# Splits of the next layer's weights moved to other steps of the vector engine, in a six-layer local-attention kernel

## The reference

```python
for i in range(DEPTH):                                   # 6
    x = attn_layer(shift_tokens(x), Wqkv[i], q_scale[i], k_scale[i], Wo[i]) + x
    x = ffn_layer(shift_tokens(x), ln_g[i], ln_b[i], W1[i], b1[i], W2[i], b2[i]) + x
```

## Time and profile before

| what | value |
|---|---|
| median of three runs | 3742.32 us |
| profiled execution, its own time | 3746.89 us |
| its span, first to last instruction | 3745.10 us |
| busy: TensorE, its weight loads, VectorE, ScalarE, GpSimd | 96%, 81%, 84%, 90%, 73% |
| mean granted TensorE clock | 0.99 |

### The profile page before, as it was taken

The page is one execution under the profiler, slowest core; times in us unless marked ns, Lnnn a source line. Parts: engine busy times, 40 slices in busy tenths (PEclk is TensorE's granted clock), DMA queues, the critical chain, the costliest instruction groups (busy, mean ns, idle before and its releaser), DMA issues.

```text
span 3745.1 us, 133069 instructions
## 1 busy us (share of the span) xinstructions
PE 3590.0 (96%) x47348; PEld 3050.9 (81%) x47348; DVE 3132.4 (84%) x7015; ACT 3369.8 (90%) x10919; POOL 2748.6 (73%) x2060
## 2 busy tenths in 40 slices
PE   7999979999999999999999999999999999999998
PEld 4666668888888888888888888888888888888887
DVE  7888978788887888888788888888888888788897
ACT  7888859989999899999899999899999999999996
POOL 0111249888788888888888788788888888888884
PEclk9999989999999999999999999999999999999999
DMA  2000001111121111111111111111111111111111
GB/s 99 7 7 16 7 21 45 35 32 34 38 49 34 37 31 32 43 43 38 32 32 38 38 45 37 32 32 39 39 44 34 32 32 44 34 35 37 40 37 38
DMA packets 164727, 132.71 MB, mean 35 GB/s; under 512 B 113901, under 2 KB 124781, under 8 KB 163821
## 3 DMA queue, kind: packets, MB, share of 16 engines
q1 hardware_dynamic: 164077, 124.19, 13.6%
HBM read 25.84 MB, written 4.19 MB: 8 GB/s over the span
## 4 chain that ended last, share of the span: by engine, by line
PE 73%; DVE 5%; ACT 5%; issue 4%; DVEq 0%; ACTq 0%; POOLq 0%; POOL 0%
PE bank L1015 10%; PE bank L971 10%; PE bank L996 8%; PE bank L1051 8%; PE bank L1035 6%; PE bank L933 4%; PE bank L934 4%; PE bank L935 4%; PE bank L894 4%; PE bank L1028 3%; ACT a_E L1343 2%; PE bank L867 2%; PE bank L869 2%; PE bank L868 2%; PE bank L947 2%
## 5 line engine op out<-in xcount | busy, mean ns | idle before, releaser
L1446 POOL TENSOR_TENSOR a_rn<-a_ssqc,a_minus_half 128x16 f32<-128x16 f32 x384 | 1113.9, 2901 | 514.9 <-DVE a_ssqc L1637 505.2
L1343 ACT ACTIVATE a_E<-bank,a_negmax 128x96 f32<-128x96 f32 x3072 | 1015.8, 363 | 23.6 <-DVE a_negmax L1586 23.0
L1467 POOL TENSOR_TENSOR a_r<-a_u,a_rn 128x512 f32<-128x512 f32 x768 | 789.7, 1049 | 0.6
L1454 POOL TENSOR_TENSOR a_PN<-a_E,a_erec 128x384 f32<-128x384 f32 x768 | 742.4, 987 | 11.5 <-PE bank L996 8.1
L1343 ACT ACTIVATION_READ_ACCUMULATOR a_E<-bank,a_negmax 128x1 f32 x3072 | 707.7, 230 | 0.0
L1326 ACT ACTIVATE a_QK<-bank 128x512 f32<-128x512 f32 x768 | 467.5, 609 | 130.2 <-PE bank L971 130.1
L1319 ACT ACTIVATE a_sq<-bank 128x512 f32<-128x512 f32 x768 | 483.9, 630 | 44.1 <-PE bank L935 12.6
L1599 DVE TENSOR_TENSOR a_u<-bank,a_rot_c 128x512 f32<-128x512 f32 x768 | 521.3, 679 | 2.4 <-ACT a_sq L1319 2.4
L1609 DVE TENSOR_TENSOR a_v<-bank,a_rot_s 128x512 f32<-128x512 f32 x768 | 521.8, 679 | 0.0
L971 PE MATMUL bank<-ident,a_r 128*128 128x128 f32 x3072 | 483.9, 280 | 18.9 <-DVE a_bias L1572 11.8
L1304 ACT ACTIVATE a_PT<-bank 128x512 f32<-128x512 f32 x758 | 479.7, 633 | 20.0 <-PE bank L996 16.3
(11 more groups left out here) (180 smaller groups left out, 8423.2 us busy)
## 6 DMA issues: line engine op xcount, KB each, us to landing
a_V_even<-a_V_odd SPq DMA_DIRECT2D x384, 128.0 KB, 2.3
a_V_even<-a_V_odd SPq DMA_DIRECT2D x192, 64.0 KB, 2.1
a_raw<-in_qkv SPq DMA_DIRECT2D x20, 384.0 KB, 3.6
a_x_sh<-X SPq DMA_DIRECT2D x48, 128.0 KB
a_V_even<-a_V_odd SPq DMA_DIRECT2D x192, 32.0 KB, 2.0
a_x_sh<-X SPq DMA_DIRECT2D x48, 127.0 KB
a_f_sh<-X SPq DMA_DIRECT2D x47, 128.0 KB
a_f_sh<-X SPq DMA_DIRECT2D x47, 127.0 KB
```

Of the source, the lines that this page charges most:

```text
L1343: ins = act.activation(E[:, s.par, k, :], scores[:, i % 2, col:col + KW], ACT.Exp, bias=negmax[:, s.par, k:k + 1], accum_out=esum[:, s.par ...
L1446: pool.tensor_tensor(rn[:, a.par, :], ssqc[:, a.par, :], minus_half[:, :], ALU.pow).then_inc(S["rn"], 1)
L1454: pool.tensor_tensor(PN[:, s.par, 2 * hp:2 * hp + 2, :].rearrange("p i (b k) -> p i b k", b=2)[:, :, :, 0:KW], spread(E[:, s.par, half, :] ...
L1467: pool.tensor_tensor(heads(r[:, a.par, half]), heads(u[:, a.par, half]), rn[:, a.par, mm * 2 * HG:(mm + 1) * 2 * HG].unsqueeze(2).to_broad ...
```

## The change

1. The low parts of the qkv weights get places of their own on VectorE (`P_LOW`): group 0 in step 4 of iteration 7 modulo 8, behind the first reciprocals; group 1 in step 5 of it, behind the first reciprocals and ahead of the add of the down product; group 2 in step 2 of iteration 0 modulo 8, behind the cosines of tile 0 and ahead of L1529; group 3 in step 4 of that iteration.
2. The high part of group 3 on ScalarE goes from the end of step 0 to the end of step 1 of iteration 0 modulo 8. Groups 0 to 2 stay.
3. The up split on ScalarE is done in two halves of 341 columns, at the ends of steps 0 and 1. That on VectorE goes from step 1 to step 4, behind the first reciprocals.
4. The bias goes from behind the norms and the up split to right behind the cosines of tile 0.

```diff
+P_SPLIT = ((0, 2), (0, 4), (0, 6), (1, 1))
+P_LOW = ((0, 4), (0, 5), (1, 2), (1, 4))
...
-    def split_at(n, p):
-
-        g = p // 2 - 1 if n % NB == NB - 1 and p in (2, 4, 6) else G - 1 if n % NB == 0 and n and p == 0 else None
...
+    def split_at(n, p, places=P_SPLIT):
+
+        for g, (first, place) in enumerate(places):
+            layer = (n + 1 - first) // NB
+            if (n + 1 - first) % NB == 0 and p == place and 0 < layer < DEPTH:
+                return layer, g
+        return None
...
 (ScalarE)
-                    act.activation(w1h[:, l % 2, :], w.w1[:, :], ACT.Copy, scale=w.cols[:, 0:1]).then_inc(S["w1_hi"], 1)
+                    if half == 0:
+                        ge(act, S["w1"], 32 * l)
+                        ge(act, S["up"], 2 * NF * NB * (l - 1))
+                    c = slice(half * DI, half * DI + DI)
+                    act.activation(w1h[:, l % 2, c], w.w1[:, c], ACT.Copy, scale=w.cols[:, 0:1]).then_inc(S["w1_hi"], 1)
...
-                if p == 0:
-                    split_up(n)
-                split_qkv(n, p)
+                if p < 2:
+                    split_up(n, p)
+                split = split_at(n, p)
+                if split:
+                    split_qkv(*split)
...
 (VectorE)
-                    dve.wait_ge(S["w1_hi"], l + 1)
+                    dve.wait_ge(S["w1_hi"], 2 * l + 2)
...
-                split = split_at(n, p)
+                split = split_at(n, p, P_LOW)
...
                 cosines(n, p, 0)
+                if p == P_BIAS:
+                    biases(n)
                 if p == P_TURN:
+                    split_qkv(n, p)
                     turned(n)
...
                 norms(n, p)
-                if p == P_BIAS:
-                    split_up(n)
-                    biases(n)
                 cosines(n, p, 1)
...
+                if p == P_GATES:
+                    split_qkv(n, p)
+                    split_up(n)
                 if p == P_GELU:
+                    split_qkv(n, p)
                     feed_forward_out(n)
...
-                split_qkv(n, p)
```

More of the change, by code:

```diff
@@ L1283, in gelu, with split_up, split_qkv @@
                     act.activation(gate[:, :, :], gate[:, :, :], ACT.Gelu).then_inc(S["gelu"], 1)
-            def split_up(n):
+            def split_up(n, half):
                 l = prepared(n)
                 if l is not None:
-                    ge(act, S["w1"], 32 * l)
-                    ge(act, S["up"], 2 * NF * NB * (l - 1))
-                    act.activation(w1h[:, l % 2, :], w.w1[:, :], ACT.Copy, scale=w.cols[:, 0:1]).then_inc(S["w1_hi"], 1)
-            def split_qkv(n, p):
-                split = split_at(n, p)
[L1294 to L1298, removed]
+                    if half == 0:
[3 more added lines that the diff above has]
+                    act.activation(w1h[:, l % 2, c], w.w1[:, c], ACT.Copy, scale=w.cols[:, 0:1]).then_inc(S["w1_hi"], 1)
+            def split_qkv(layer, g):
+                act.wait_ge(S["v"], (layer * NB - 1) * NP + 2 * g + 2)
+                act.wait_ge(S[f"raw{g % 2}"], 16 * (2 * (layer - 1) + g // 2 + 1))
+                high_weights(act, A, raw[:, g % 2, :], g).then_inc(S["w_hi"], 1)
             def probs(t, hp):
@@ L1575, in split_qkv @@
             def split_qkv(n, p):
-                split = split_at(n, p)
+                split = split_at(n, p, P_LOW)
                 if split:
-                    layer, g, count = split
+                    layer, g = split
                     dve.wait_ge(S["w_hi"], G * layer + g + 1)
```

## The result

The changed kernel takes 3711.51 us in the median of four runs (3706.48 to 3714.63), the kernel before 3743.61 with its fourth run. The forecast was 3708.7, in a range of 3700 to 3720. The ratio measured is 0.9911, with a 95% interval of 0.9899 to 0.9922 (the two medians alone give 0.9914). The profiled execution took 3711.75 us, its span is 3710.0.

What follows compares the result with a forecast made beforehand. TensorE, 96% busy, was taken to bound the kernel, so work costs only where it delays TensorE. 6.51 us a layer, five times 32.6, plus 1.0 at the start gave 33.6 off the 3742.32 median: 3708.7, range 3700 to 3720.

Steps and rivals of the forecast that it cites:

- Bounds and ceiling: TensorE's delays set the time; excess of 5.20, 2.24 and 1.62 us, 9.06 a layer, 45.3 in all, besides the start.
- Iteration 4 modulo 8: Bias earlier: TensorE's wait of 2.35 us and slow-clock stretch of 1.70 go, shift matmuls' 1.25 stays; 3.95 us taken.
- the shift matmuls might be what brings the clock down: Rival, iteration 4 modulo 8: clock falls despite the bias's move; 5 x 1.70 = 8.5 us, 3717; chance 0.06.
- Iteration 7 modulo 8: VectorE's splits 0 and 1 fit waits in steps 4 and 5, split 2 leaves step 6: 2.24 - 0.4 = 1.84 us.
- The 0.4 us left to the rotations: End of step 6: part of the 0.94 us wait that stays, between 0.07 and 0.94, with TensorE waiting for the sines.
- Iteration 0 modulo 8 and the new place of split 2: Split 3 off step 0 gains 1.50 us; split 2 in step 2 waits for GpSimd's product, costing 0.78, bounds 0 to 1.8.
- ScalarE's splits 0 to 2 keep their places, 3 goes one step later ... Nothing for each: Queues term: ScalarE's qkv splits, with group 3's one step later, cost nothing.
- ScalarE has waits for TensorE in nearly every step, so nothing: Iteration 4 modulo 8: the second fixed part from halving ScalarE's up split costs nothing.
- ScalarE as the one that was late: Rival: ScalarE's splits, four a layer at 0.89 us, are each on the path; 17.8 us less gain, 3726; chance 0.09.
- The running power: Rival: GpSimd's 2.90 us power blocks VectorE's splits; step 5's add 1.25 us late, 6.3 in all, 3715; chance 0.06.
- Queues: SP queue loads the third group behind split 0, some 7 us later; ScalarE needs it at least 16 us later; nothing.
- Start: Iteration 0's up split, 1.73 us in a VectorE chain, moves to step 4: gain 0 to 1.7 us, 1.0 taken.

Runs made afterwards that it cites:

- the bias alone: The kernel before with only the bias moved behind the first cosines, the up split staying whole in step 1: ratio 0.9951, iteration 20 66.55 us.
- qkv part alone: The changed kernel with bias and up splits as before, so only the qkv splits' places differ from the kernel before: ratio 0.9957.
- up split later only: The kernel before with VectorE's up split alone moved to step 4, the bias staying behind the norms: ratio 0.9956, iteration 20 68.13 us.

## Why the prediction was right, point by point

- **Bounds and ceiling.** TensorE sets the time, and the excess of three iterations of eight is what the change can get. The excess of 9.1 us a layer is 2.6 now (1.33, 0.52 and 0.76, counted from 65.28). Of the 1.33 the halves are 0.15, and the shift matmuls at most the other 1.18, less than the 1.25 of their row. The differences measured below are between two executions whose ordinary iterations differ by 0.08 us. Each counted from its own, they are 3.87, 1.74 and 0.86: 6.47 us a layer, where 6.51 was forecast.
- **Iteration 4 modulo 8:** 3.95 us forecast, 3.95 measured; the bias alone gave 4.01, so that the last hundredths are chance. The two halves of the mechanism, the wait of 2.35 and the slow stretch of 1.70, measured 2.35 and 1.6; their sum is the 3.95. That the shift matmuls might be what brings the clock down was a rival with 0.06, and fell.
- **Iteration 7 modulo 8:** 1.84 forecast, 1.82 measured (67.62 to 65.80). The 0.4 us left to the rotations came by the way that was named: the transposes of step 7 start 0.37 us behind the matmul ahead of them (0.12 in iteration 21), 0.15 behind the end of the low x, and the next projection 0.14 late, behind the sines. In all 0.52 us are left. But the prediction took the whole excess of 2.24 us for reachable and named a wait for only 0.94 of it. The rest was for the most part the wait of 0.93 us that split 1 caused at the down product, through ScalarE. Moving split 1 took it away, though the prediction gave only a hole that it fits, not a wait that it ends: here the number was better founded than the reasons given for it.
- **Iteration 0 modulo 8 and the new place of split 2:** 1.50 less 0.78 is 0.72 forecast, 0.94 measured. The step that failed is "ScalarE's splits 0 to 2 keep their places, 3 goes one step later ... Nothing for each". Group 3's new step costs a wait of 0.47 us, the longest TensorE has in that iteration. The chain for split 2 was right in kind, a wait behind the running product and then behind the sines, but it was priced too high: 0.51 us where ScalarE's delay is gone, and some 0.2 where TensorE is late already. That the sum came near is luck: a cost that was left out and one that was put too high nearly make up for each other. For the same reason "ScalarE has waits for TensorE in nearly every step, so nothing" was wrong by 0.15 us for the halves: the wait it has ahead of the copy is 0.23 or 0.24 us in steps 1 and 2 of iteration 21. The instruction behind the second half starts 0.47 us after it, the one behind group 3's high part 0.73 us. Less the wait that is 0.23 and 0.49, and TensorE waits 0.20 and 0.47 us for the copy.
- **ScalarE as the one that was late** had 0.09 and a price of 17.8 us. At one place of the four it is so: ScalarE has no wait left there while TensorE waits for it, which was a sign named for being wrong, and it costs 0.35 us.
- **The running power:** no block in any of the runs: 0.92 and 0.93 us beside a power of 2.90. Beside products a split took 1.39 us, and the unit products 2.75 for 2.04. The Trainium skill (SBUF — State Buffer, "Who interferes with whom") has a VectorE instruction with two SBUF inputs contend with a GpSimd instruction that reads SBUF, for an exclusive lock. The runs agree with it beside products, and not beside a power.
- **Queues:** the third group's load goes out at 2043.23, 7 us later in its iteration than before, and ScalarE takes up the group at 2063.87 without a wait. That part of the term was nothing, as forecast.
- **Start:** 1.0 forecast, 3.6 and 2.4 measured in two executions. The term was undersized; it counted a chain on VectorE and left out the clock. Iteration 0 from its first add to its last, kernel before, changed kernel, changed kernel again:

```profile
526.43:572.65 46.22, 37.58 (x388) 30.77 (x388) 41.06 (x65) 31.27 (x103) 39.84 (x28) 0.85 0.15 34
...
530.34:572.96 42.62, 33.73 (x396) 26.95 (x395) 40.84 (x66) 31.71 (x104) 39.67 (x28) 1.00 0.16 36
...
535.48:579.33 43.85, 35.93 (x388) 28.96 (x388) 40.17 (x65) 31.59 (x104) 39.74 (x28) 0.92 0.16 35
```

The last two are one kernel: 1.23 us between them go with the clock alone. How much of the rest is the shorter chain on VectorE, which the prediction counted, and how much the clock that follows from it, no run separates.

- **The total.** The median came to 3711.51 us, 2.8 over the forecast, the gain to 32.1 instead of 33.6. That is closer than the terms deserve. The layers became 39.0 us shorter in the profiled executions, not 33.6: 5 x 0.2 from iteration 0 modulo 8, 2.6 from the start, and some 2 from ordinary iterations that took 65.29 instead of 65.35. The rest of the span went the other way, since the first attention, which the change does not touch, ended 3.9 us later. The run medians hold all of that. Measured again, on another chip, they are 35.2 us apart (3748.55 and 3713.34).

## What to carry to other kernels

In a pipeline with one engine at its limit, price a piece of work by the hole that it is put in. Look for the row of that engine whose idle time stands in brackets, go back from there in the queue of the releaser, and move the small thing that is waited for ahead of the large thing that is not. If the named waits do not add up to the excess of an iteration, as in iteration 7 modulo 8 here, another wait is still to be found. A piece that is only shifted by a step on a nearly full engine has to be priced with the same care as the one that the change is about. And when several delays reach one step, undo them one at a time and together, for one alone may show nothing.

## What the runs showed that was not expected

A wait of TensorE of 2.35 us was followed by a stretch at a mean granted clock of 0.73 to 0.77 over 6.3 us in nine of ten cases (all five of the kernel before, four of the five of the qkv part alone) and by 1.00 in the tenth; the waits of 0.94 us (kernel before) and 1.51 us (up split later only) by 1.00. The price of the fall, 1.6 us, is two thirds of that of the wait itself. What decides the tenth case is open. Open too is why ordinary iterations take 65.29 us in some executions and 65.35 in others, of the same kernel.
